# One attention branch of a graph layer: ones in the heads' last columns, rows normalized by ScalarE, node value and bias added with the mixing

## The reference

```python
xn = _layernorm(x)                                   # rows: mean and variance over 256 features, eps 1e-5
x = x + segment_sum(edge_weight * xn[src], dst) + node_vec1 + mix(xn)
x = x + ffn(_layernorm(x))                           # 8 experts, 2 per node

def mix(seq):                                        # 4 heads of 64 features
    q, k, v = (split_heads(seq @ w.T) for w in (wq, wk, wv))
    k = _layer_norm(k, ln_k_g, ln_k_b)               # over the 64 features of a head
    v = _layer_norm(v, ln_v_g, ln_v_b)
    kv = einsum('bhsd,bhse->bhde', k, v) / S         # one 64 x 64 matrix per head, summed over all nodes
    ga = einsum('bhsd,bhde->bhse', q, kv)            # back to (S, 256)
    return ga @ wo.T + bo
```

## Time and profile before

| | us |
|---|---|
| median of 3 runs | 2285.6 (2284.03 to 2287.64) |
| the profiled execution | 2287.49 |
| its span, first to last instruction | 2285.7 |
| front | 0 to 178 |
| sorting and mixing | 178 to 305 |
| aggregation, then experts | 305 to 2285.7 |

### The profile page before, as it was taken

One profiled execution on the slowest core, in us unless ns is written; L12 is line 12 of the kernel. 1 busy time (PEld: TensorE's weight loads), 2 busy tenths in 40 slices (PEclk: granted clock), 3 DMA queues, 4 the chain that ended last, 5 costly groups with the idle time before them and its releaser, 6 DMA issues. The chain is left out here.

```text
span 2285.7 us, 45562 instructions
## 1 busy us (share of the span) xinstructions
PE 2101.8 (92%) x16549; PEld 1849.5 (81%) x16550; DVE 1958.9 (86%) x3342; ACT 1177.3 (52%) x1696; POOL 1613.5 (71%) x1364
## 2 busy tenths in 40 slices
PE   7996789999999999999999999999999728999993
PEld 4665678888888888888888888888789618999992
DVE  7998999999999999999999999999778595555552
ACT  2225655555545555555554555554223157888771
POOL 3770067777777777777777777777777347888873
PEclk9997999999999999999999999999999868999996
DMA  4542433333223333332233233332445454555555
GB/s 140 156 121 76 129 113 91 91 89 102 89 90 100 93 93 90 102 94 92 91 102 90 89 90 101 93 92 87 133 130 155 155 140 78 82 83 81 82 81 140
DMA packets 160929, 235.87 MB, mean 103 GB/s; under 512 B 54834, under 2 KB 121805, under 8 KB 160490
## 3 DMA queue, kind: packets, MB, share of 16 engines
q0 software_dynamic: 70896, 164.43, 27.9%
q1 hardware_dynamic: 75536, 55.29, 8.4%
q10 hardware_dynamic: 14314, 13.68, 1.8%
HBM read 186.46 MB, written 53.24 MB: 105 GB/s over the span
## 5 line engine op out<-in xcount | busy, mean ns | idle before, releaser
L816 POOL DMA_INDIRECT picked<-xn_dram,place x1029 | 1185.8, 1152 | 435.6 <-issue 302.5
L914 PE MATMUL bank<-picked,pick_w 128*128 128x256 f32 x2058 | 504.1, 381 | 16.4 <-DMA picked<-xn_dram,place 15.8
L1026 ACT COPY stage<-bank 128x512 f32<-128x512 f32 x343 | 200.9, 586 | 548.4 <-PE bank L902 542.5
L914 PEld LDWEIGHTS bank<-picked,pick_w 128*128 128x128 f32 x2058 | 386.5, 190 | 85.4 <-issue 34.9
L910 PE MATMUL bank<-window,stage 128*128 128x256 f32 x1568 | 382.7, 387 | 0.0
L1287 DVE TENSOR_TENSOR hot_w<-hots,cur 128x1536 bf16<-128x1536 bf16 x343 | 328.6, 958 | 11.9
L980 ACT COPY field_rep<-fields 128x1666 bf16<-128x1666 bf16 (+1 forms) x193 | 322.4, 1675 | 1.2 <-DVE vals L1163 1.2
L910 PEld LDWEIGHTS bank<-window,stage 128*128 128x128 f32 x1568 | 283.6, 191 | 30.7
L1283 DVE TENSOR_TENSOR hots<-ends,cur 128x1408 bf16<-128x1408 bf16 x343 | 303.4, 885 | 1.7 <-ACT cur L1020 1.7
L902 PE MATMUL bank<-hot_w,hots 128*128 128x128 bf16 x4116 | 285.9, 219 | 4.4 <-issue 3.5
L910 PE MATMUL bank<-stage 128*128 128x256 f32 x1176 | 286.0, 386 | 0.0
(11 more groups left out here) (255 smaller groups left out, 3386.7 us busy)
## 6 DMA issues: line engine op xcount, KB each, us to landing
picked<-xn_dram,place POOLq DMA_INDIRECT x1029
w<-in_L_ffn_W_dram SPq DMA_DIRECT2D x16, 512.0 KB, 10.0
xn_dram<-xn ACTq DMA_DIRECT2D x49, 128.0 KB, 1.9
xT_dram<-xT ACTq DMA_DIRECT2D x49, 128.0 KB, 2.1
base_dram<-acc SPq DMA_DIRECT2D x7, 896.0 KB, 7.8
sum_dram<-acc SPq DMA_DIRECT2D x7, 896.0 KB, 4.6
z_dram<-vals SPq DMA_DIRECT2D x7, 896.0 KB, 8.5
out_dram<-sum_dram SPq DMA_DIRECT2D x1, 6250.0 KB, 21.8
```

The costliest lines, as they stand in the source:

```text
L816: pool.indirect_dma_start(out=picked[:, i % SETS * PICK + q, :], out_offset=None, in_=xn_dram, in_offset=bass.IndirectOffsetOnAxis(ap=plac ...
L914: mm = pe.matmul(sum_ps[pp], pick_w[i % SETS][:, q, :], picked[:, i % SETS * PICK + q, :], start=False, stop=(q == PICK - 1))
L1026: act.copy(block_sb[pp].rearrange("p j c -> p (j c)"), banks[pp][:, :]).then_inc(a_copied, 1)
```

## The change

- The last column of each head of 64 in `hat` is set to one, once. The projected rows are centred, so a head's last feature is minus the sum of its others; the products with ones give the sums that the 129th column and the one-column matmuls gave. `kv_product` is two matmuls of 128 columns.
- Gains, offsets and the spreading of the last feature go into `wo` and `wq` by two small basis matrices (`patterns`, `bases`, `center_wq`, matmuls at tiles 9 and 12, copies `take_wo` by ScalarE). `kv()` in the second stage only divides by N.
- `normalize` moves from VectorE to ScalarE (activation with scale and bias; GpSimd makes the bias, `center`), behind `take_xT` in its order, with four rooms of xn (`ROOMS`) instead of three.
- `heads` squares the 256 key columns in one instruction and each of the four value heads in one of its own that also writes the sum of the squares. VectorE's reduction covers the keys alone.
- `shift` goes. `add_mix` adds the node value as well; `bo` is added to row 0 of M. For that the first row of the first half of every xT tile in SBUF is ones: GpSimd sets it once, and `load_xT` loads around it in two transfers.
- The gains and offsets of keys and values are loaded as columns, eight small transfers, ahead of the edge windows on SP's queue instead of four behind them.

```diff
@@ front @@
+    ROOMS = DEPTH + 1
 sp:
+            with nc.allow_non_contiguous_dma(reason="one value per partition"):
+                for i, v in enumerate((kg, kb, vg, vb)):
+                    for h in range(P // HD):
+                        sp.dma_start(col[h * HD:(h + 1) * HD, i:i + 1], v.rearrange("(d a) -> d a", a=1)).then_inc(w_in[1], 16)
             for n in range(NT):
...
 gpsimd, chunk_root:
+                pool.wait_ge(rstd_done, 2 * c + 1)
+                pool.wait_ge(var_done, 2 * c + 2)
+                pool.tensor_tensor(center[c % 2][:, :], mean[c % 2][:, :], rstd[c % 2][:, :], ALU.mult).then_inc(rstd_done, 1)
 scalar:
+            def normalize(t):
+                c, i = divmod(t, UN)
+                if i == 0:
+                    act.wait_ge(rstd_done, 2 * (c + 1))
+                if t >= ROOMS:
+                    act.wait_ge(stored[t % ROOMS], 16 * (t // ROOMS))
+                    act.wait_ge(turned, t + 1 - ROOMS)
+                act.activation(xn[t % ROOMS][:, :], acc[:, t, :], ACT.Identity, bias=center[c % 2][:, i:i + 1], scale=rstd[c % 2][:, i:i + 1]).then_inc(xn_done, 1)
...
             def heads(t):
                 act.wait_ge(proj, t + 1)
                 if t >= 2:
                     act.wait_ge(summed, t - 1)
-                act.activation(sq[t % 2][:, :], proj_ps[t % 4][:, :], ACT.Square).then_inc(squared, 1)
+                    act.wait_ge(hvar_done, t - 1)
+                act.activation(sq[t % 2][:, 0:D], proj_ps[t % 4][:, 0:D], ACT.Square).then_inc(squared, 1)
+                for h in range(H, HH):
+                    at = slice(h * HD, (h + 1) * HD)
+                    ins = act.activation(sq[t % 2][:, at], proj_ps[t % 4][:, at], ACT.Square, accum_out=ss[t % 2][:, h:h + 1])
+                ins.then_inc(squared, 1)
...
+            def take_wo(n):
+                act.wait_ge(w_turned, n + 3)
+                act.copy(woT[:, :, :].rearrange("p k d -> p (k d)"), side_ps[:, :]).then_inc(w_ready, 1)
...
                 if t + DEPTH < NT:
                     take_xT(t + DEPTH)
+                if t + ROOMS < NT:
+                    normalize(t + ROOMS)
 tensor, kv_product:
-                    pe.matmul(kv_ps[c][:, 0:P + 1], hat[t % 2][0:rows, 2 + c, 0:P], hat[t % 2][0:rows, c, :],
-                              start=(t == 0 and c == 0), stop=(t == LAST), skip_group_check=True)
-                    mm = pe.matmul(kv_ps[c][:, P + 1:P + 2], hat[t % 2][0:rows, c, 0:P], hat[t % 2][0:rows, c, P:P + 1],
-                                   start=False, stop=(t == LAST), skip_group_check=True)
+                    keys, values = (hat[t % 2][0:rows, at:at + P // HD, :].rearrange("p h d -> p (h d)") for at in (c * (P // HD), H + c * (P // HD)))
+                    mm = pe.matmul(kv_ps[c], values, keys, start=(t == 0 and c == 0), stop=(t == LAST), skip_group_check=True)
 tensor, loop over t:
+                if t == 9:
+                    pe.wait_ge(w_ready, 6)
+                    for c in range(2):
+                        mm = pe.matmul(side_ps[:, c * D:(c + 1) * D], basis[1][:, :], woT[:, c, :], start=(c == 0), stop=(c == 1), skip_group_check=True)
+                    mm.then_inc(w_turned, 1)
...
 vector, one:
-                dve.wait_ge(squared, t + 1)
-                dve.tensor_reduce(ss[t % 2][:, :], sq[t % 2][:, :].rearrange("p (h d) -> p h d", d=HD), AX.X, ALU.add).then_inc(summed, 1)
+                dve.wait_ge(squared, 2 * t + 1)
+                dve.tensor_reduce(ss[t % 2][:, 0:H], sq[t % 2][:, 0:D].rearrange("p (h d) -> p h d", d=HD), AX.X, ALU.add).then_inc(summed, 1)
                 dve.wait_ge(summed, t + 1)
+                dve.wait_ge(squared, 2 * t + 2)
                 dve.tensor_scalar(hvar[t % 2][:, :], ss[t % 2][:, :], 1.0 / HD, EPS, ALU.mult, ALU.add).then_inc(hvar_done, 1)
-                if t + DEPTH < NT:
-                    normalize(t + DEPTH)
-                    shift(t + DEPTH)
@@ edge_sum @@
             def load_xT(c):
...
-                to = picked[:, 0:BU, :] if c % 2 else stage[:, 0:BU * D].rearrange("p (t d) -> p t d", d=D)
-                sp.dma_start(to, of).then_inc(xT_in[c % 2], 16)
+                to = xT_room[c % 2]
+                sp.dma_start(to[1:P, :, :], of[1:P, :, :]).then_inc(xT_in[c % 2], 16)
+                sp.dma_start(to[0:1, :, P:D], of[0:1, :, P:D]).then_inc(xT_in[c % 2], 16)
 gpsimd:
+            for i in range(2):
+                pool.memset(xT_room[i][0:1, :, 0:P], 1.0).then_inc(small_in, 16)
 tensor, matrix:
+                    if m == 0:
+                        pe.matmul(mix_ps[m], ident[0:1, :], bo_row[0:1, :], start=False, stop=True)
 vector, add_mix:
-                dve.tensor_tensor(acc[:, t, :], acc[:, t, :], mix_ps[t % 4], ALU.add).then_inc(mix_added, 1)
+                dve.scalar_tensor_tensor(out=acc[:, t, :], in0=acc[:, t, :], scalar=nv[:, t:t + 1], in1=mix_ps[t % 4], op0=ALU.add, op1=ALU.add).then_inc(mix_added, 1)
 vector: key_sums and the old kv are gone (thirteen operations); left of kv:
+                        ins = dve.tensor_scalar(kvT[at, c, at], kv_ps[c][at, at], 1.0 / N, None, ALU.mult)
```

## The result

The changed kernel takes 2507.99 us (median of 4 runs, 2507.1 to 2511.77) against 2284.82 us for the kernel before (4 runs, 2280.93 to 2287.64): ratio 1.0964, 95% interval 1.0944 to 1.0983. It is 223 us slower; I had said 2493 us. The profiled execution has a span of 2505.3 us (before 2285.7), and the granted clock is 0.93 on average instead of 0.97.

What follows compares the result with a forecast made beforehand. The front was taken as bound by steps waiting for each other, the second stage after the change by xT loads on one engine. 2285.6 + 30 (front) + 177 (loads) = 2492.6, say 2493 us, range 2390 to 2560.

Steps and rivals of the forecast that it cites:

- a ring: Front: squares, xT copy and projection wait for each other, 2.93 us a round; this, not an engine's load, is the bound.
- The number of rounds: Front: 45 rounds from the squares at 24.94 (tile 3) to those at 172.44 (tile 48), 147.5 us.
- The squares: Front, ScalarE: five squares instructions instead of one make a round 0.94 us longer, +42 us over 45 rounds.
- late rounds: Front: rounds delayed by late `hat`, TensorE's counting or half clock cost 15.5 us; 11 of them go.
- The start: Front: 2 us gained, as ScalarE can normalize while VectorE still prepares weights.
- Small parts: Normalization covered by the projection's 2 us; second stage: adds 3.3 us more, key-value chain 2 to 3.5 less, together nothing.
- The divisor step: Second stage: engines used are the largest divisor of the row count up to 16; 127 rows get one, 37.5 us a load.
- A + 78.5: Second stage: A is the first issue of an xT load; `wg`, queued behind two loads, lands 78.5 us later.
- Different engines: Rival, second stage: xT loads run on different engines, +84 us instead of +177, 2400 us; chance 8%.
- Wide or hidden loads: Rival, second stage: xT loads stay wide or hidden and cost nothing, 2316 us (2286 to 2360); chance 14%.
- TensorE's weight loads as the bound: Rival, front: TensorE's weight loads, not ScalarE, set the 2.93 us; with wide xT loads 2253 us, faster; chance 3%.
- Clock: Rival, front: idler TensorE may drop to 1.2 GHz, +54 us at worst; one case in ten within the forecast.

Runs made afterwards that it cites:

- e9: Changed kernel with its 127-row loads cut into 112 and 15 rows and the four squares written without sums, VectorE reducing all heads; ratio 1.0063 to the kernel before.
- e2: Changed kernel with its 127-row loads cut into 112 and 15 rows, one 512-column square and VectorE's whole reduction put back; ratio 1.0003 to the kernel before.
- e7: Kernel before without the one-column matmuls (key sums), except in the last tile; ratio 1.0003 to the kernel before.
- e6: Kernel before with each xT load issued as rows 1 to 127 and row 0, both in full width; ratio 1.0751 to the kernel before.
- e4: Changed kernel with the xT loads of chunks 1, 3 and 5 issued by GpSimd instead of SP; ratio 1.0632 to the kernel before.

## Why the prediction was right, and where its steps were off

**The bound.** That a ring and not an engine sets the front's pace held: the changed kernel (3.54 = the three steps), e9 and e2 move with the squares-to-copy time and e7 doesn't move with TensorE's work.

**The number of rounds was wrong.** The squares at 24.94 are the third of 49, tile 2 counted from 0, and not tile 3: to 172.44 there are 46 rounds. That leaves 12.7 us of late rounds, not 15.5.

**The squares were priced too high.** Predicted 0.27 + 4 x 0.29 = 1.43 us, measured 0.28 + 4 x 0.197 = 1.07. The form was right (two overlapped instructions a head), the size of one was 0.10 and not 0.145: each starts 0.10 us behind the one before, less than the 0.12 of the earlier trace rows. 46 x 0.61 = +28 us instead of +42.

**Late rounds.** From the third to the last square the changed kernel takes 164.1 us, 1.2 more than 46 x 3.54. So 11.5 of 12.7 us went. I had 11 of 15.5: the amount came out, the share did not.

**The start** was forecast 2 us earlier and came 5.8 us later (third square at 30.69). TensorE's first transposes wait for the weights `wk` and `wv`, which land at 17.0 us instead of 11.6, though SP issues them at the same 2.74 and 3.33 us. In the eight kernels with the changed front they land at 15.9 to 17.1 us, in the four with the front of before at 9.2 to 11.6. What of the change's other early loads delays them was not tried; one candidate is ScalarE's load `dst_s`, which leaves at 3.53 us instead of 4.08 since two small loads ahead of it are gone. Sum of the front: +28.1 - 11.5 + 5.8 - 0.2 = +22.2, predicted +30.

**Small parts.** Normalization takes 0.60 us on ScalarE (0.4 to 0.5 forecast) and lies in the projection's 2 us, as said. The three-operand add takes 0.48 us, as said. With the loads hidden and one square (e2) the rest of the change shows no difference that these runs can tell.

**The loads.** The divisor step held: one engine, 24 GB/s, the same engine for each. The sum fell short: +194.3 us against +177. From 240 to 270 us the engine moves 692 rows of 1 KB:

```profile
DMA packets 692, 0.71 MB, mean 24 GB/s; under 512 B 2, under 2 KB 692, under 8 KB 692
```

That is 43.4 ns a row and 38.6 us a load of 889 rows. My 24.2 GB/s, from four slices of the earlier trace rows, gave 37.5 and was 3% too high; over the five later loads this is 5 us. Nothing was lost between loads: 889 rows and 56 of a store make 41.0 us, and the chunks come every 40.95.

The first mixing matmul is at A + 82.3 instead of A + 78.5. SP could issue `wg` only at 275.06 us, but the second load was still running then, so `wg` did stand behind it on the engine, as forecast; the transfers of SP's queue end at 281.7 and the matmul starts at 282.69. Of the 3.8 us 2.2 are the rate of the two loads and 0.9 the time from the first issue to the first row. The third load leaves at A + 97.4 instead of A + 92; 1.6 us of that lie between the first mixing matmul and the end of the chunk's adds (granted clock 0.87, 0.48 us an add).

From there to the last chunk's matmuls it takes 209.2 us instead of 198.4: four chunk pitches of 41 us and one of 45.3. The last load met GpSimd's first twelve gathers. From 478 to 496 us:

```profile
q0 software_dynamic: 573, 1.57, 29.3%
q1 hardware_dynamic: 323, 0.33, 5.3%
picked<-xn_dram,place POOLq DMA_INDIRECT x12
```

SP's queue (q1) moves 323 rows, where 43.4 ns a row make 415: 4.0 us lost. I had said that the gathers do not suffer, and had not asked what they take from the load; e6 has the same last pitch (45.3). The last 0.9 us lie between the last chunk's matmuls and its first add.

**The sum.** That 2493 came within 15 us of 2508 is partly luck: the front was forecast 8 us too long and the loads 17 us too short.

**Rivals.** Different engines (2400 us): excluded for SP's loads, which follow each other at 24 GB/s; with a second issuer (e4) it held for the later pairs and not for the first. Wide or hidden loads: excluded by the windows. TensorE's weight loads as the bound: excluded by e7. Clock: the front kept 1.00; in the long waits it fell to 0.50 (240 to 270 us) and TensorE mixed more slowly, which was covered by the next load.

## What to carry to other kernels

Before a load is cut, look at the row counts of the pieces: taking one row of 128 away cost 194 us over seven loads here, and cutting the 127 rows into 112 and 15 gave it back. Before an engine's work is made lighter, put one round in order of time and see which steps wait for each other; work moved off two full engines onto an idle one made each round 0.6 us longer, because that one stood in the ring. And when a ring is opened, list the queues that had been ahead thanks to it.

## What the runs showed of the hardware

- A square of 64 columns with an accumulated sum is two instructions on ScalarE, and each costs 0.10 us of start to start; without the sum four took 0.41 us.
- Behind a transfer that runs on one engine SP's next issue on the queue is held until nearly all of it is through: 34.9 us for the first, 38.4 with the second behind it, 13 to 16 us for 106 rows on two engines. Everything else that SP has to issue, `wg` and the windows here, waits as well.
- A one-engine load shares its engine with whatever else is in flight: a wide store added 56 rows (2.4 us) to each, and twelve gathers made the last load 4 us longer.
- A load of 127 rows issued by GpSimd cost GpSimd 7.3 us of issuing and ran on one engine too, in packets of four rows. With SP's load on the same engine the two alternated packet by packet (115 to 114), and SP's load got a fifth of its pace; a later one ran beside SP's, at 21 and 19 GB/s. From its issue until TensorE could go on it took 51.8 us.
